# Attention stage of a fused hybrid kernel: moved half-steps, residuals, centring, value copies and third norm, and the balancing's mid-step reciprocal behind both masks

## The reference

```python
x = x + dcnv2(_gn(x), ...)                      # deformable 3x3 convolution
x = x + _L1_conv_ref(_gn(x), ...)               # 3x3 convolution, mixed by gates and a balanced 4x4 matrix
t = _to_tokens(x)                               # 8 images x 256 tokens x 64 channels
t = t + _L2_attn_ref(_ln_t(t), ...)             # causal attention, 8 heads of 64
t = t + _L2_ffn_ref(_ln_t(t), ...)              # 8 experts, top 2, gelu
t = t + _L3_attn_ref(_ln_t(t), ...)             # gated window mean of 16 tokens
t = t + _L3_ffn_ref(_ln_t(t), ...)              # 16 experts, top 2, silu
# the balanced matrix of the second convolution block, per image:
def sinkhorn_knopp(H_tilde, t_max=20):
    M = jnp.exp(H_tilde)
    for _ in range(t_max):
        M = M / jnp.sum(M, axis=-1, keepdims=True)
        M = M / jnp.sum(M, axis=-2, keepdims=True)
    return M
```

## Time and profile before

| | |
|---|---|
| median of 3 runs | 480.04 us (478.22 to 480.06) |
| profiled execution | 478.49 us, of which the span from first to last instruction is 476.7 us |
| PE busy | 437.0 us (92%) |
| DVE busy | 348.0 us (73%) |
| ACT busy | 282.1 us (59%) |
| GpSimd busy | 174.8 us (37%) |
| mean granted TensorE clock | 0.977 of 2.4 GHz |
| first mask of attention starts | 134.76 us |
| first expert matmul | 277.42 us |

### The profile page before, as it was taken

One profiled execution on the slowest core, in us unless ns is written; L12 is line 12 of the kernel. 1 busy time (PEld: TensorE's weight loads), 2 busy tenths in 40 slices (PEclk: granted clock), 3 DMA queues, 4 the chain that ended last, 5 costly groups with the idle time before them and its releaser, 6 DMA issues.

```text
span 476.7 us, 9083 instructions
## 1 busy us (share of the span) xinstructions
PE 437.0 (92%) x2982; PEld 303.7 (64%) x2982; DVE 348.0 (73%) x1090; ACT 282.1 (59%) x677; POOL 174.8 (37%) x304
## 2 busy tenths in 40 slices
PE   6998999999878988979999999999998888898996
PEld 4786777766467887969898954344444544445553
DVE  5288989867777657886988864637667879887673
ACT  3478766533557877747788876765674243343441
POOL 4400002203134563382884333415351354443441
PEclk9999999999989998979999999999999989999899
DMA  7300000000400000012120004112112122132141
GB/s 178 149 2 2 1 1 0 1 2 0 89 3 1 1 2 1 2 36 55 41 49 2 2 3 152 56 40 69 44 44 87 52 65 72 45 112 79 54 137 25
DMA packets 13567, 20.94 MB, mean 44 GB/s; under 512 B 4592, under 2 KB 6384, under 8 KB 13008
## 3 DMA queue, kind: packets, MB, share of 16 engines
q1 hardware_dynamic: 12896, 19.92, 14.8%
q10 hardware_dynamic: 624, 0.43, 0.3%
HBM read 19.62 MB, written 0.72 MB: 43 GB/s over the span
## 4 chain that ended last, share of the span: by engine, by line
PE 63%; DVE 19%; issue 6%; ACT 6%; POOL 3%; DMA 1%; SPq 0%; DVEq 0%; ACTq 0%; POOLq 0%
PE PS L2189 14%; PE PS L1885 7%; PE PS L1923 6%; PE PS L2200 5%; PE PS L2211 5%; PE PS L1944 3%; PE PS L2109 2%; PE PS L2121 2%; PE PS L2012 2%; PE PS L1843 2%; DVE QL L1477 2%; PE PS L2027 2%; DVE score_arena L1586 2%; PE PS L2059 2%; DVE prod L1332 1%
## 5 line engine op out<-in xcount | busy, mean ns | idle before, releaser
L2189 PE MATMUL PS<-YTs,WH 64*128 64x512 f32 x192 | 79.5, 439 | 1.1 <-ACT VV L1071 0.7
L2189 PE MATMUL PS<-YX,WH 64*128 64x512 f32 x192 | 79.5, 438 | 0.0
L735 POOL TENSOR_TENSOR pr<-pr 128x512 f32<-128x512 f32 x38 | 49.1, 1291 | 68.2 <-DVE pr L1639 42.3
L968 ACT ACTIVATE score_arena<-score_arena,nmx 128x128 f32<-128x128 f32 (+1 forms) x128 | 56.9, 446 | 22.4 <-DVE nmx L1586 21.9
L1071 ACT ACTIVATE VV<-PS 128x512 f32<-128x512 f32 x64 | 35.3, 594 | 46.9 <-PE PS L2189 46.8
L2189 PEld LDWEIGHTS PS<-YTs,WH 64*128 64x128 f32 x192 | 36.3, 189 | 29.9 <-ACT VV L1071 11.4
L1024 ACT ACTIVATE stage<-PS,wk 128x512 f32<-128x512 f32 x64 | 40.8, 684 | 21.6 <-PE PS L2189 21.4
L1752 DVE TENSOR_TENSOR stage<-VV,PS 128x512 f32<-128x512 f32 x64 | 41.7, 682 | 15.8 <-ACT VV L1071 10.1
L908 ACT ACTIVATE st_mem<-PS 128x512 f32<-128x512 f32 x72 | 36.9, 609 | 19.4 <-PE PS L1923 19.3
L2121 PE MATMUL PS<-cst,score_arena 128*128 128x128 f32 x192 | 34.1, 288 | 6.2 <-ACT score_arena L968 5.8
L2109 PE MATMUL PS<-YTs,QH 128*128 128x128 f32 (+1 forms) x128 | 39.0, 329 | 0.0
(11 more groups left out here) (280 smaller groups left out, 1130.0 us busy)
## 6 DMA issues: line engine op xcount, KB each, us to landing
QH<-gate_store SPq DMA_DIRECT2D x96, 128.0 KB, 2.9
stage<-in_wexp SPq DMA_DIRECT2D x6, 512.0 KB, 6.1
wk<-in_w SPq DMA_DIRECT2D x1, 1034.0 KB, 8.3
wa<-in_wat SPq DMA_DIRECT2D x1, 768.0 KB, 6.5
cst<-in_consts SPq DMA_DIRECT2D x1, 483.0 KB, 5.1
out<-X SPq DMA_DIRECT2D x14, 32.0 KB, 1.9
wc<-in_w SPq DMA_DIRECT2D x2, 183.5 KB, 5.1
score_arena<-in_wcv SPq DMA_DIRECT2D x2, 144.0 KB, 5.2
```

The source lines that it names most:

```text
L735: nc.gpsimd.tensor_tensor(acc[:, c % 2], acc[:, c % 2], weighted[:, u % 2], ALU.add).then_inc(acc_added, 1)
L968: ins = nc.scalar.activation(PR[:, s % 3, cols], MS[:, s % 3, cols], ACT.Exp, bias=nmx[:, s % 3, qt:qt + 1], scale=-1.0, accum_out=rsum[:, ...
L2189: ins = mm(PS[:, banks[i], :], w[hs, m, tiles[i] * P:(tiles[i] + 1) * P], ys[i][hs, cs], start=(k == 0), stop=(k == 2))
```

## The change

Six edits, none of which adds or removes work, but for which engine does half-steps 8 and 9.

1. `DVE_HALVES` is 8: GpSimd now does half-steps 8 and 9 too, in its assisted form, so that the balancing has 32 half-steps inside the attention loop (17 steps with a mid-step reciprocal, 15 with one at the end). The four that DVE does ahead of attention are spread: 4 ahead of `add_conv(2)`, 5 between the two query remainders, 6 and 7 behind them.
2. In each step the mid-step reciprocal stands behind both masks.
3. `second_residual(2)` and `(3)` stand right behind the copy of the trace in step 19, ahead of the query remainder of that step.
4. ACT copies v(3,0) ahead of `copy_probs(19)` in step 20, and v(4,0) ahead of the exponentials of step 30.
5. `ln_center(3)` of step 29 stands ahead of that step's query remainder.
6. `ln_out(3)` moves from step 32 to step 34.

```diff
-DVE_HALVES = 10
+DVE_HALVES = 8
-MID_INVERSE, END_INVERSE = [s for s in range(17) if s != 4], [s for s in range(15) if s != 3]
+MID_INVERSE, END_INVERSE = [s for s in range(18) if s != 4], [s for s in range(16) if s != 3]
...
             for s in range(STEPS + 1):
+                if s == 30:
+                    project(("v", 4, 0))
                 if s < STEPS:
...
                     ins.then_inc(probs_ready, 1)
+                if s == 20:
+                    project(("v", 3, 0))
                 if s >= 1:
                     copy_probs(s - 1)
                 if s < STEPS:
                     for name in attention_fills(s):
-                        if name[0] in ("q", "v"):
+                        if name[0] in ("q", "v") and (s, name[2]) not in ((20, 0), (30, 0)):
                             project(name)
...
             ln_evac("yA", 0)
+            half_steps(1, 4, 5)
             add_conv(2)
             add_conv(3)
...
                 if name[0] == "q":
                     query_remainders(name)
-            half_steps(1, 4, DVE_HALVES)
+                    if name[2] == 0:
+                        half_steps(1, 5, 6)
+            half_steps(1, 6, DVE_HALVES)
             take_tokens(1)
...
                         dve.wait_ge(misc_free, FILL["cB", 0] + 1)
+                        second_residual(2)
+                        second_residual(3)
...
                                                ALU.add, ALU.min, nmx[:, s % 3, 0:1])
+                nc.vector.tensor_tensor_reduce(MS[:, s % 3, P:3 * P], PS[:, s % 2, P:3 * P], c_("causal"), -SCALE, 1e30,
+                                               ALU.add, ALU.min, nmx[:, s % 3, 1:2]).then_inc(masked_ready, 1)
                 if s in MID_INVERSE:
                     inverse()
-                nc.vector.tensor_tensor_reduce(MS[:, s % 3, P:3 * P], PS[:, s % 2, P:3 * P], c_("causal"), -SCALE, 1e30,
-                                               ALU.add, ALU.min, nmx[:, s % 3, 1:2]).then_inc(masked_ready, 1)
+                if s == 29:
+                    ln_center(3)
                 if s >= 1:
                     take_fills(s - 1)
-                if s == DIAG_AT + 1:
-                    second_residual(2)
-                    second_residual(3)
...
-                if s in (2, 21, 29):
-                    ln_center({2: 1, 21: 2, 29: 3}[s])
+                if s in (2, 21):
+                    ln_center({2: 1, 21: 2}[s])
...
-                if s in (5, 24, 32):
-                    ln_out({5: 1, 24: 2, 32: 3}[s], False)
+                if s in (5, 24, 34):
+                    ln_out({5: 1, 24: 2, 34: 3}[s], False)
```

## The result

The changed kernel takes **465.81 us** (median of 4 runs, 464.41 to 467.98), the kernel before 479.52 (4 runs). The ratio is 0.9722, 95% interval [0.9678, 0.9766]. The profiled execution took 466.17 us with a span of 464.4, against 478.49 and 476.7.

What follows compares the result with a forecast made beforehand. No engine alone was the bound: PE held 63% of the chain, DVE 19%. From 478.49 us, -3.8 - 1.6 - 3.6 = -9.0 gave 469.5; the median was put at 470.0, range 466.8 to 474.5 (8 in 10).

Steps and rivals of the forecast that it cites:

- the price of PE's clock: Lulls of steps 19-21 and 29-34: 2.4 GHz likelier kept at both, but only 1.95 of 3.35 us taken.
- behind step 36 all should shift as a whole: Behind step 36, order untouched: PE-bound steps and expert blocks shift as a whole, with no further gain in the sum.
- the full ends: Low end of the range, 466.8 us: all parts at their full ends, -10.4, and 1.3 for spread of runs.
- part A: Balancing, steps 0 to 16: earlier first mask and fewer late reciprocals, -3.8 us, bounds -1.7 and -4.2.
- Part B: Steps 19 to 23: residuals and copy of v(3,0) moved into waits, -1.6 us, bounds -1.05 and -2.1.
- Part C: Steps 29 to 36: centring, copy of v(4,0) and third norm moved, -3.6 us; -4.5 with clock kept, -2.2 without.
- the norm used GpSimd's power, whose input and order do not change: Third norm, moved to step 34: its power was taken as unchanged, and the norm gives back about 1.2 us there.
- Rival 1: Clock still falls at both lulls, steps 19-21 and 29-34: gain 7.05 us, about 472 us; chance 14%.
- rival 2: Balancing still sets the pace at its end, two half-steps cost 2.07: gain 5 to 7, 472 to 475 us; chance 9%.
- rival 3: Bunched masks lengthen each balancing round trip, 1.7 us per 0.1 of score delay beyond cover: slower kernel; chance 3%.
- rival 4: The waits filled are filled by something else, releases come later: within 0.5% of before; chance 4%.
- The bound on SBUF contention: GpSimd's added short products beside DVE's work: nothing added; by the skill's rule up to 1.2 us lost.

Runs made afterwards that it cites:

- x6b: Kernel before, nothing reordered, with 6 and 11 dummy matmuls in PE's waits of steps 20 and 30; 472.71 us, ratio 0.9882.
- z: The changed kernel run again, unaltered; 464.71 us, ratio 0.9707 to the kernel before.
- x1b: Kernel before with half-steps 8 and 9 on GpSimd, DVE's four spread, and the mid-step reciprocal behind both masks; 472.23 us, ratio 0.9874.
- x2: Kernel before with only half-steps 8 and 9 moved to GpSimd and DVE's four spread; 476.81 us, ratio 0.9936.
- x3: Kernel before with only the mid-step reciprocal moved behind both masks; 475.34 us, ratio 0.9932.
- x8: Changed kernel with the third norm put back in step 32; 470.33 us, ratio 0.9837 to the kernel before.
- x4: Kernel before with only the residuals of step 19 and the copy of v(3,0) moved ahead; 478.14 us, ratio 0.9979.
- x7: Changed kernel with the copy of v(4,0) back behind step 30's exponentials and copy of probabilities; 468.16 us, ratio 0.9776 to the kernel before.
- x6: Kernel before, nothing reordered, with 14 and 24 dummy matmuls at PE's waits of steps 20 and 30; 476.82 us, ratio 0.9966.

## Why the prediction was wrong in size

**The step that failed is the price of PE's clock.** The prediction held 7.05 us of waits (3.8 + 1.05 + 2.2) and 1.95 of clock. It had worked out 3.35 for the clock and took a little over half of it, because it had placed engines by hand; and it said that behind step 36 all should shift as a whole, which puts low stretches in the expert blocks at nothing. From one profiled execution to the other the gain is 12.3 us, 3.3 more than its 9.0. By the traces these are:

- 1.2 for the clock inside attention: x6b shows about 3.1 for the two falls, where 1.95 was taken. The full 3.35 would have been near.
- 0.8 in the expert blocks (203.94 to 203.14 us from step 63 on), where one low stretch fewer came; the sum had no term for it.
- 1.3 for the waits: 11.5 us won in attention, less 3.1, are 8.4, where 7.05 was forecast.

So 2.0 of the 3.3 are clock. That the expert blocks gave 0.8 and not 0 or 3.1 is luck of the execution, as z shows.

The runs without a trace point the same way, more roughly. The 46 runs of the kernel before that were taken beside the experiments have a mean span of 476.8 us and a mean clock of 0.9764, so they lack 11.2 us of full clock; ten runs of the changed kernel have 463.6 and 0.9957, and lack 2.0. If attention won 11.5 in all of them, as in the two traces, 1.7 of the 13.2 us of span lie in the expert blocks, and the clock gave about 4.8 (3.1 + 1.7; an estimate). Within one kernel, runs that lack 1 us more are 0.73 us longer (0.59 in the kernel before, 1.03 in the changed one); by that slope it would be 9.2 x 0.73 = 6.7 (5.4 to 9.5). The slope is an average and also counts the stretch from 136 us, which cost nothing. Either way the clock gave over twice the 1.95.

The range failed for the same reason: its low end allowed the full ends and 1.3 of spread, nothing for the clock behind step 36. Its -10.4 also holds part A at 3.8; with that part's own bound of 4.2 the range would have begun at 466.4, still above the result.

- **Part A**, forecast -3.8 with a bound of -4.2, measured -4.26 by step 19 (4.65 in x1b). The start was 2.05 in the forecast, 1.91 in the trace; the late reciprocals 1.6, in the trace 1.72 (34.61 - 32.89). The end was too small: 0.2 to 0.4 were forecast to be handed over, 0.64 were (3.62 earlier at step 15, 4.26 at step 19). By x2 and x3 that is 0.3 paid for the two added half-steps and about 0.8 won by edit 2 (1.6 earlier at step 15, 2.33 at step 19).
- **Part B**, forecast -1.6 with a bound of -2.1, measured -2.23. Its wait part was 0.81 at step 20 (forecast 0.8) and about 1.0 by step 22 (forecast 1.05); the clock gave 1.2. But x1b kept that clock without edit 3. The 1.2 belongs to whichever edit moves the lull or shortens it, and only once.
- **Part C**, forecast -3.6 with a bound of -4.5, measured -5.0. The way there came as worked out with the clock kept: 5.05 won by step 34 (forecast up to 4.9), 1.1 given back by the norm (1.2), 1.1 regained by step 36. What the prediction did not see is what each move is worth. It gave the copy of v(4,0) the leading part and saw in the norm's move only the 1.2 that it costs at its new place. Taken back from the finished kernel, the copy is worth 0.7 and the norm's move 3.8. The step that misled was "the norm used GpSimd's power, whose input and order do not change": with the rest mended, the norm's turn on DVE comes 11.0 us earlier in x8 (213.04 - 0.35 against 205.08 - 3.43), its power only 8.0, and the wait grows from 0.35 to 3.43.
- **Rival 1** (clock still lost at both) did not come, and its "2.20 of 4 busy was already too little" does not hold by itself: x1b had 2.20 and kept the clock; **rival 2** neither (the last reciprocal is at 169.22, the mask of step 18 at 170.51); **rival 3** is refuted by x3: 33.12 us for 28 intervals, against 34.61; **rival 4** (within 0.5% of before) by the result.
- The bound on SBUF contention, 0 for GpSimd's short products, held: the reciprocals' ordinary interval is 1.03 before and after. For long instructions it does not hold (next section), but the residuals' extra 0.65 fell into a wait.

What stays open is why the clock falls behind a stretch in one moment and not behind the same stretch 2 or 4 us earlier. The runs show that it is so, not what decides it. So it is also open how much of the clock kept at the two places is owed to the shorter waits, and how much to their new moments; the two traces of the changed kernel, 1.4 us apart, both kept it.

## What to carry to other kernels

Price a move twice: by the wait that it shortens, and by PE's lull that it mends. If a lull has a low clock behind it, take the full price of that stretch, and widen the range for low stretches elsewhere that a shift in time can add or drop. The span of a single trace can't rank versions that differ by under 3 us (one program gave 464.4 and 460.7 here), but what is won between two steps repeated to 0.03 us. When a stall is removed, ask of each instruction behind it whether its input comes earlier too. Here, undoing one move at a time from the finished kernel showed what adding edits to the old one hid.

## What the runs showed of the hardware

- **What a fall of the clock costs depends on who sets the pace where it lies.** The kernel before has a clock of 0.65 from 136 to 140 us, x2 has 1.00 there, and x2 wins nothing from step 2 to step 15 (2.54 and 2.63 earlier), since the balancing sets the pace. In x4 it lasts until 144.5 us instead of 140.6, up to where the balancing waits for a variance, and costs 1.0. In x7 it lies from 131.8 to 135.2 us, ahead of the first scores, and costs 0.8 (7.24 us from the copy of the first transposes to the first mask, 6.44 in the changed kernel). At steps 22 and 31 to 34 it costs 1.2 and 1.95. The Trainium skill, "TensorE: Matmul & The Clock Gate", section "HAM oscillation — how this bites in real kernels", tells of idle gaps, each a wait for DMA, behind which the array is throttled and the next work starts cold. The falls behind PE's waits of 1.80 and 3.00 us agree in kind, with waits for ACT in place of DMA. That the same wait of 1.80 was followed by no fall in x1b, that section does not say. The prediction drew from it that a gap shortened but not closed may pay nothing for the clock: here 0.78 us were left at both places, and the clock stayed.
- **DVE and GpSimd slow each other in long SBUF instructions.** The residuals took 1.52 us beside GpSimd's products (2.74 us for three of 128x512, 2.62 alone) and 0.87 alone. The norm took 2.36 beside GpSimd's subtraction and 1.12 alone, and three of the eight subtractions took 0.77 to 0.93 us beside it, where one takes 0.73. The Trainium skill, "SBUF — State Buffer", section "SBUF: two separate sides", says that a VectorE instruction with two SBUF inputs and a GpSimd one that reads SBUF take a shared pair of ports for a whole instruction, while the other waits. The trace agrees that they hold each other up, the norm's cast with its one SBUF input too (0.71 against 0.29). It shows this as longer records, 1.7 to 2.4 times as long on DVE, and not as idle time.
- A dummy matmul of 128x128 in f32 took 0.23 us in x6 and 0.24 in x6b (24 in 5.52 us, 11 in 2.62), cheap enough to bridge a known wait: x6b gained 1.2% in this kernel, about half of it inside attention, where the dummies stand.
